# Per-token attention products: full-array block-diagonal stationary against 32x32 pieces of TensorE

## What is computed

```python
q = (h @ wq.T + bq).reshape(B, S, 32, 32)      # k, v alike
scores = jnp.einsum('bshd,bstd->bsht', q, k) / np.sqrt(32)
probs = jax.nn.softmax(scores, axis=-1)
context = jnp.einsum('bsht,bstd->bshd', probs, v).reshape(B, S, 1024)
x = x + context
x = x + ffn(layernorm(x))                      # base product + 2-of-8 experts of rank 16
```

## Time and profile before

| | before |
|---|---|
| span of the profiled execution | 1543.5 us |
| three timed executions, median | 1545.02 us (1543.29 to 1545.65) |
| PE busy | 1367.9 us (89%) |
| DVE busy | 1261.1 us (82%) |
| ACT busy | 503.8 us (33%) |
| POOL busy | 210.7 us (14%) |
| one loop step (two starts of k1, at 839.13 and 883.92 us) | 44.79 us |

### The profile page before, as it was taken

The page is one execution under the profiler, slowest core; times in us unless marked ns, Lnnn a source line. Parts: engine busy times, 40 slices in busy tenths (PEclk is TensorE's granted clock), DMA queues, the critical chain, the costliest instruction groups (busy, mean ns, idle before and its releaser), DMA issues.

```text
span 1543.5 us, 30006 instructions
## 1 busy us (share of the span) xinstructions
PE 1367.9 (89%) x12432; PEld 750.4 (49%) x12432; DVE 1261.1 (82%) x1751; ACT 503.8 (33%) x572; POOL 210.7 (14%) x280
## 2 busy tenths in 40 slices
PE   0777999999999999999999999999999999999996
PEld 0444445545544554554455455445545544554553
DVE  5778888888888888888888888888888888888874
ACT  7952222333222233322223332222333222233320
POOL 0011110011111001111100111110011111001110
PEclk9989999999999999999999999999999999999997
DMA  9401111000111100011110101111000111100000
GB/s 380 165 1 42 41 41 37 31 29 25 41 41 41 37 31 29 25 41 41 41 35 33 31 23 41 41 41 36 32 31 24 41 41 41 38 30 30 24 29 28
DMA packets 20208, 70.52 MB, mean 46 GB/s; under 512 B 2144, under 2 KB 3168, under 8 KB 20192
## 3 DMA queue, kind: packets, MB, share of 16 engines
q1 hardware_dynamic: 20192, 70.30, 12.8%
HBM read 53.51 MB, written 16.78 MB: 46 GB/s over the span
## 4 chain that ended last, share of the span: by engine, by line
DVE 61%; PE 14%; issue 10%; ACT 6%; DVEq 5%; DMA 3%; SPq 0%; POOL 0%; ACTq 0%; POOLq 0%
DVE work L308 6%; DVE work L800 6%; DVE x_lo L684 5%; PE acc L965 5%; DVE work L725 5%; PE acc L976 5%; DVE work L872 4%; DVE work L843 4%; DVE work L718 4%; DMA work<-x_dram 3%; DVE work L794 3%; DVE work L889 3%; DVE work L911 3%; DVEq L751 3%; DVE work L906 2%
## 5 line engine op out<-in xcount | busy, mean ns | idle before, releaser
L1018 PE MATMUL acc<-base_parts,x_hi 128*128 128x512 f16 x1024 | 325.0, 381 | 32.4 <-DVE work L308 32.4
L956 PE MATMUL attn_ps<-work 128*128 128x32 f16 x2048 | 329.0, 177 | 2.7 <-DVE work L718 1.7
L957 PE MATMUL attn_ps<-work 128*128 128x32 f16 x2048 | 327.3, 176 | 0.0
L958 PE MATMUL attn_ps<-work 128*128 128x32 f16 x2048 | 326.9, 176 | 0.0
L957 PEld LDWEIGHTS attn_ps<-work 128*128 128x128 f16 x2048 | 189.7, 96 | 201.6
L308 ACT COPY work<-work 32x2048 f16<-32x2048 f16 x96 | 182.1, 1897 | 139.2 <-DVE work L718 88.3
L956 PEld LDWEIGHTS attn_ps<-work 128*128 128x128 f16 x2048 | 193.7, 96 | 6.0 <-issue 3.6
L965 PE MATMUL acc<-w_hi_k,x_hi 128*128 128x512 f16 x512 | 140.6, 385 | 62.1 <-DVE work L718 28.4
L1018 PE MATMUL acc<-base_parts,x_lo 128*128 128x512 f16 x512 | 194.4, 380 | 0.0
L958 PEld LDWEIGHTS attn_ps<-work 128*128 128x128 f16 x2048 | 188.9, 96 | 0.0
L668 DVE BATCH_NORM_STATS2 stats<-work 128x6 f32<-128x512 f32 x128 | 82.3, 685 | 126.4 <-DMA work<-x_dram 125.3
(11 more groups left out here) (135 smaller groups left out, 2231.4 us busy)
## 6 DMA issues: line engine op xcount, KB each, us to landing
work<-x_dram SPq DMA_DIRECT2D x64, 512.0 KB, 3.5
out_dram<-work SPq DMA_DIRECT2D x32, 512.0 KB, 2.8
work<-wT_dram SPq DMA_DIRECT2D x19, 512.0 KB, 9.5
v_parts<-wT_dram SPq DMA_DIRECT2D x8, 512.0 KB, 14.8
base_parts<-wT_dram SPq DMA_DIRECT2D x5, 512.0 KB, 12.1
biases_sb<-bias_dram SPq DMA_DIRECT2D x4, 512.0 KB, 15.2
work<-agT_dram SPq DMA_DIRECT2D x1, 544.0 KB, 4.7
lora_up<-lora_b_dram SPq DMA_DIRECT2D x1, 512.0 KB, 15.8
```

Of the source, the lines that this page charges most:

```text
L956: nc.tensor.matmul(dst, diag[:, i, 0, :], moving[:, i, 0, :], start=True, stop=False)
L957: nc.tensor.matmul(dst, diag[:, i, 0, :], moving[:, i, 1, :], start=False, stop=False)
L958: return nc.tensor.matmul(dst, diag[:, i, 1, :], moving[:, i, 0, :], start=False, stop=True)
L1018: nc.tensor.matmul(dst, rows_part[:, m // 3, :], w_part[:, m // 3, cols], start=(m == 0), stop=False)
```

## The change

The block-diagonal stationary goes. q and v have split tiles of their own (`q_parts`, `vt_parts`), the copies of `spread_quadrant` and their semaphores go, and `attend_one` issues twelve matmuls for a token group: for each of the three products of parts, one for each quadrant, with a 32x32 stationary and 32 moving columns, reading partitions of that quadrant and writing the same partitions of PSUM. A tile's scores are 384 such matmuls, its context 384. They no longer stand between wide matmuls: the scores come behind the last wide matmul of `dense(0)`, the context behind the last of q0.

```diff
-        def spread_quadrant(copy, g, ready):
-
-            s = slice(g * QD, (g + 1) * QD)
-            copy(diag[s, :, :, s], parts[s, :, :, :]).then_inc(ready, 1)
...
-            nc.gpsimd.memset(work[:, 0:block_diag_len], 0.0).then_inc(diag_zero, 1)
+            nc.gpsimd.memset(expert_no[:, 0:1], 0.0).then_inc(diag_zero, 1)
...
-                nc.scalar.copy(parts[:, :, 0, :], turned3).then_inc(q_hi_ready, 1)
...
-                for g in Q_ACT:
-                    spread_quadrant(nc.scalar.copy, g, qdiag_ready)
+                nc.scalar.copy(q_parts[:, :, 0, :], turned3).then_inc(q_hi_ready, 1)
...
-                low_part(t, q_hi_ready, q_lo_ready)
...
-                for g in Q_DVE:
-                    spread_quadrant(nc.vector.tensor_copy, g, qdiag_ready)
+                low_part(t, q_parts, q_hi_ready, q_lo_ready)
...
-                dve.wait_ge(v_lo_ready, t + 1)
-                for g in V_DVE:
-                    spread_quadrant(nc.vector.tensor_copy, g, vdiag_ready)
...
-                dst = attn_ps[:, i * QD:(i + 1) * QD]
-                nc.tensor.matmul(dst, diag[:, i, 0, :], moving[:, i, 0, :], start=True, stop=False)
-                nc.tensor.matmul(dst, diag[:, i, 0, :], moving[:, i, 1, :], start=False, stop=False)
-                return nc.tensor.matmul(dst, diag[:, i, 1, :], moving[:, i, 0, :], start=False, stop=True)
+                fixed = q_parts if moving is k_parts else vt_parts
+                terms = ((0, 0), (0, 1), (1, 0))
+                for n, (fixed_part, moving_part) in enumerate(terms):
+                    for g in range(NQ):
+                        s = slice(g * QD, (g + 1) * QD)
+                        mm = nc.tensor.matmul(attn_ps[s, i * QD:(i + 1) * QD], fixed[s, i, fixed_part, :],
+                                              moving[s, i, moving_part, :], start=(n == 0),
+                                              stop=(n == len(terms) - 1))
+                return mm
...
                 for k in range(KC):
                     nc.tensor.matmul(dst, x_hi[:, k, :], w_hi[g][:, k, cols], start=(k == 0), stop=False)
-                    if moving is not None:
-                        attend_one(moving, first + k)
...
                 if attended is not None:
+                    for i in range(QD):
+                        small = attend_one(moving, i)
                     small.then_inc(attended, 1)
...
-                    if moving is not None:
-                        for i in range(m * QD // steps, (m + 1) * QD // steps):
-                            small = attend_one(moving, i)
                 if moving is not None:
+                    for i in range(QD):
+                        small = attend_one(moving, i)
                     small.then_inc(scored, 1)
```

More of the change, by code:

```diff
@@ L131, in block_kernel @@
         stage = work[:, 0:KC * HID].rearrange("p (k n) -> p k n", k=KC)
-        diag = carve(block_diag_len).bitcast(F16).rearrange("p (t a c) -> p t a c", t=QD, a=2)
+        pair = dict(t=QD, a=2)
+        q_parts = carve(HID).bitcast(F16).rearrange("p (t a c) -> p t a c", **pair)
+        vt_parts = carve(HID).bitcast(F16).rearrange("p (t a c) -> p t a c", **pair)
+        carve(block_diag_len - 2 * HID)
         soft = carve(HID)
@@ L566, in step @@
                 act.wait_ge(vt_ready, t + 1)
-                act.wait_ge(qdiag_ready, NQ * (t + 1))
-                nc.scalar.copy(parts[:, :, 0, :], turned3).then_inc(v_hi_ready, 1)
+                if prev:
+                    act.wait_ge(ctx_acc, t)
+                nc.scalar.copy(vt_parts[:, :, 0, :], turned3).then_inc(v_hi_ready, 1)
                 if prev:
                     gate_exp(t - 1)
-                act.wait_ge(v_lo_ready, t + 1)
-                act.wait_ge(scored, t + 1)
-                spread_quadrant(nc.scalar.copy, V_ACT[0], vdiag_ready)
                 act.wait_ge(shifted, t + 1)
@@ L913, in step @@
                     finish(t - 1, 0)
-                low_part(t, p_hi_ready, p_lo_ready)
+                low_part(t, parts, p_hi_ready, p_lo_ready)
                 if prev:
@@ L953, in attend_one, with project @@
             def attend_one(moving, i):
-                dst = attn_ps[:, i * QD:(i + 1) * QD]
-                nc.tensor.matmul(dst, diag[:, i, 0, :], moving[:, i, 0, :], start=True, stop=False)
-                nc.tensor.matmul(dst, diag[:, i, 0, :], moving[:, i, 1, :], start=False, stop=False)
-                return nc.tensor.matmul(dst, diag[:, i, 1, :], moving[:, i, 0, :], start=False, stop=True)
-            def project(t, g, n, bank, done, any_low, moving=None, first=0, attended=None):
+                fixed = q_parts if moving is k_parts else vt_parts
[7 more added lines that the diff above has]
+                return mm
+            def project(t, g, n, bank, done, any_low, moving=None, attended=None):
                 cols = slice(n * HALF, (n + 1) * HALF)
@@ L978, in project @@
                         mm.then_inc(done, 1)
-                    if moving is not None:
-                        small = attend_one(moving, first + KC + k)
                 if attended is not None:
+                    for i in range(QD):
+                        small = attend_one(moving, i)
                     small.then_inc(attended, 1)
@@ L1033, in context_ready @@
             def context_ready(p):
-                pe.wait_ge(vdiag_ready, NQ * (p + 1))
+                pe.wait_ge(v_lo_ready, p + 1)
                 pe.wait_ge(p_lo_ready, p + 1)
@@ L1055, in step @@
                     context_ready(t - 1)
-                project(t, "k", 1, 1, k_acc, any_low[0], moving=parts if prev else None)
+                project(t, "k", 1, 1, k_acc, any_low[0])
                 if prev:
@@ L1062, in step @@
                     pe.wait_ge(w_lo_done, (Q_ + 1) * KC)
-                project(t, "q", 0, 2, q_acc, any_low[0], moving=parts if prev else None, first=2 * KC,
+                project(t, "q", 0, 2, q_acc, any_low[0], moving=parts if prev else None,
                         attended=ctx_acc if prev else None)
@@ L1091, in step @@
                 pe.wait_ge(k_lo_ready, t + 1)
-                pe.wait_ge(qdiag_ready, NQ * (t + 1))
+                pe.wait_ge(q_lo_ready, t + 1)
                 if prev:
```

20 lines of the change are left out of this document (3 added, 17 removed).

## The result

The changed kernel takes 1903.68 us (median of four, 1901.33 to 1914.21), the kernel before beside it 1545.34. The ratio is 1.233 [1.230, 1.236]: slower by 23%. The number is Rival 1's to a microsecond, and that is chance: its mechanism is not there.

The account below looks back on a forecast made before the run. DVE's order was taken to tie PE at 44.79 us a step; after the change PE binds at 36.9 + 2A = 45.3. 31 steps by 0.55 plus 1.8 in the tail, on 1543.5, gave 1564 us timed; range 1500 to 1905.

Parts of the forecast that it names:

- Rival 1: Pieces in the small blocks go one after another, 25 ns apart: block 9.6 us, step 56.1 us, 1903 us; chance 0.26.
- The sum: Whole kernel: 31 steps by 0.55 us, plus 1.8 in the tail, on 1543.5 give 1562, timed 1564 us.
- p = 11 ns: Distance between starts of 32x32 matmuls in the small blocks: 11 ns, geometric middle of 6.25 and 20.
- Rival 2: Four quadrants share one slot in the small blocks: 6.25 to 9 ns a matmul, 1474 to 1517 us; chance 0.22.
- A: Time of one block of 384 small matmuls, scores or context: taken as 4.2 us, against 2.4 before.
- The loop's instructions are kept: PE's loop of 427 pairs is kept, not fetched again; the forecast adds no fetching cost for the changed loop's 1003.
- The clock: Granted clock in the loop, now 2.4 GHz: a fall to 1.2 would double wide matmuls and make every sum wrong.
- Rival 3: PE waits for instructions: loop not kept, three packets of 2.2 us a block, step 50.3 us, 1716 us; chance 0.10.
- the 36.2: PE's work in one loop step without attention: 36.2 us.
- The changes wide to small: Four changes a step between wide and small matmuls drain PE, 0.17 us each: 0.7 us a step.
- The collision of L800: L800 takes 2.83 us beside POOL's L407, 1.28 with POOL idle; a context block over about 3.8 us avoids the collision.

Follow-up runs that it names:

- kernel of 907 pairs: Changed kernel without the loop's never executed branches and without the high x low product for 12 of 32 context token groups; 1671.82 us (one run).
- kernel of 827 pairs: Changed kernel without the loop's never executed branches and without the high x low product for all 32 context token groups; 1511.16 us, 0.979.
- 875 pairs: Changed kernel without the loop's never executed branches and without the high x low product for 20 of 32 context token groups; 1519.61 us (one run).
- POOL's wait: Half changed kernel (scores by pieces behind dense(0)'s first wide matmul, context block-diagonal), POOL's low part of k now waiting for the residual addition; 1480.33 us, 0.958.
- body of 955 pairs: Changed kernel without the loop's never executed branches for products with low parts of the weights; 1919.53 us, 1.243.
- long block-diagonal loop: Kernel before, its never executed branches lengthened so that the loop's body has 1003 pairs; 1621.39 us, 1.050.

## Why the prediction was wrong, step by step

**Direction.** Slower was called right, for a wrong reason, so by luck. The sum's result of 1564 and the range's upper end at Rival 1 have nothing to do with what happened.

**p = 11 ns: wrong.** Three kernels without stops show 8.1 to 8.2 ns, Rival 2's case, and the first pieces of a block, four in 25 ns, its lower end. The middle between "one after another" and "four at once" was a choice without a row; the nearest rows bounded it and could not place it. With 8.1 ns, A is 3.1 us and the sum gives 36.9 + 6.2 = 43.1 a step. The Trainium skill (TensorEngine Tiling (Array Packing), Instruction Overhead) would have had each matmul pay its 60 cycles. The trace disagrees for pieces: three of them start in that time, and four at the start of a block.

**"The loop's instructions are kept": the step that failed.** I gave it one chance in ten and 1716 us. It happened: nine packets an iteration. The price was off too: A was to be three packets at 2.2 us each, 6.7 in all, and it is 3.1 us of pieces with two full stops on top, 7.7 in the step shown and 8.1 in the mean. My own figures (1003 pairs against a program of 1473 that had been loaded once) did not show that it was kept; I read the small packet count of a 427-pair loop as comfort for one over twice as long.

**The clock, named only as what would break every sum: it broke.** Some 115 us of 356. The mean of 0.986 was treated as a property of the kernel that the change leaves alone. In the kernel of 907 pairs the blocks without stops keep the clock and those with stops lose it. Rival 3 should have carried it in its price: with what was measured since, its sum is 36.6 + 6.1 + 10.0 + 3.7 = 56.4 us a step and 1905 in all, near the measured 1904. That is hindsight: none of these terms but the 36.2 stood in a row of before.

**The changes wide to small: 0.7 us a step predicted, 0.4 measured.** From the last wide matmul (1024.39 + 1.89 - 0.38 = 1025.90) to the first piece at 1026.21 it is 0.31 us in the change, 0.09 more than 0.216; the way back takes 0.12 (1033.95 to 1034.07). Four changes are 0.4. Right in kind, and small only because there are four.

**The collision of L800: right in kind, its bound too high.** 1.28 us with A over 3.8, as predicted. With a context block of 256 pieces (2.1 us, the kernel of 827 pairs) the median is 2864 ns, with 304 pieces (2.5 us, 875 pairs) 2499, and with 336 in the kernel of 907 pairs 1284, in the iterations without stops too. So some 2.8 us can be enough, though there each such iteration follows one with stops; no run has a whole context block of 3.1 us without them. The remedy of its own, POOL's wait, was worth 9.6 us, 1489.89 to 1480.33.

**Was the direction sure?** Kept whole, the change would hardly have been slower. From the kernel with 875 pairs at 1519.6 (one run), the 2560 pieces that it leaves out add 2560 x 8.1 ns = 21 us: an estimate of 1540, within a few tenths of a per cent of before. It is the upper end, because that kernel still waits for the second normalisation (22.5 us in 25 steps, 28 in 31), and that wait shrank from 1.3 to 0.9 us a step when the context's block grew from 256 to 304 pieces. If the wait went altogether, the estimate would be 1512. PE's own work is shorter by 2 us a step in either case.

**Open.** Why the clock is low for longer with a body of 955 pairs than with 1003; how much of the 77 us of the long block-diagonal loop (1621.39 against 1543.98) belongs to jumps; what sets the pitch of 8.3 ns behind the 32nd piece; and why stops of up to 1.8 us between full-array matmuls leave the clock up.

## What to carry to other kernels

Count the instructions of a loop's body before splitting a matmul into pieces: a step over what the engine keeps turns a kept loop into a fetched one, and short instructions are the ones that can't hide the fetching. A small count of instruction packets says only that the present body fits, never how near it is. And a stop of PE can cost twice, once itself and once in the clock behind it (310 and 115 us here), so look at the granted clock behind every stop; it did not fall behind the stops of the long block-diagonal loop.

## What had not been expected of the hardware

Four 32x32 pieces on four quadrants share a slot: the first 32 pieces of a block go at four in 25 ns, where full-array matmuls of the same 32 columns start 25 ns apart each. A long block goes at 8.1 to 8.2 ns a piece, 33 ns for four. A packet of 16 KB holds 256 instructions; 18 to 22 packets in a run mean a kept loop, 149 one that is fetched every second iteration (907 pairs), 286 one fetched always (1003). The limit of a kept body lies between 875 and 907 pairs. A fetched loop stops PE 1.9 to 2.8 us a packet when it issues a pair in 8 ns. Behind such a block the granted clock is 0.50 for about eight wide matmuls; behind the same block without stops they follow each other at full speed. Stops of up to 1.8 us between full-array matmuls left the clock at 1.00.
